# One quarter of every tile keeps its ninth product in PSUM, TensorE adds two planes to it and ScalarE takes it out; the hand-set course gets new places

## The reference, cut to what matters

```python
x = x + _L0_conv_ref(_gn(x), ...)      # x is 32 x 64 x 56 x 56, float32
x = x + _L1_conv_ref(_gn(x), W, b)

def _L0_conv_ref(x, dw_weight, ...):    # residual = x
    h = sign(x);  h = depthwise 3x3 conv with sign(dw_weight)
    h = sign(bn1(prelu1(h)));  h = 1x1 conv with sign(pw_weight)
    return bn2(prelu2(h)) + residual

def _L1_conv_ref(x, W, b):              # "involution", K = 3
    filters = einsum('bchw,oc->bohw', x, W) + b      # nine filters per channel and pixel
    patches = the nine 3x3 shifts of x
    return sum(patches * filters over the nine)
```

## Time and profile before

| what | number |
|---|---|
| median of three runs | 725.28 us (723.54 to 725.59) |
| the profiled execution, its time | 727.71 us |
| its span, first to last instruction | 725.8 us |
| DVE busy | 659.6 us, 91% |
| POOL busy | 636.0 us, 88% |
| PE busy | 608.0 us, 84% |
| ACT busy | 499.9 us, 69% |
| mean granted TensorE clock | 0.98 of full speed |

### The profile page before, as it was taken

How to read it: one execution, slowest core, us unless ns; L and a number is a source line. 1 busy time by engine, 2 the same in 40 slices (tenths; PEclk the granted TensorE clock), 3 DMA queues, 4 the chain that set the end, 5 groups by cost and what they waited for, 6 DMA issues and landing times.

```text
span 725.8 us, 18653 instructions
## 1 busy us (share of the span) xinstructions
PE 608.0 (84%) x8001; PEld 258.9 (36%) x8001; DVE 659.6 (91%) x984; ACT 499.9 (69%) x627; POOL 636.0 (88%) x330
## 2 busy tenths in 40 slices
PE   2649789889898988898898988888888889898777
PEld 1324333333334333343433333343333334342313
DVE  4939889999999999999999999999989999999986
ACT  6957896868778596868769696867849686735100
POOL 2003589999999999999999999999989999999997
PEclk9969999999999999999999999999999999999999
DMA  5246596998999899898989899898979987898974
GB/s 204 82 136 109 100 269 150 190 244 186 253 196 252 187 217 234 166 259 186 267 181 248 191 205 230 186 256 189 257 162 207 226 186 166 185 202 172 205 157 136
DMA packets 34279, 142.10 MB, mean 196 GB/s; under 512 B 3348, under 2 KB 11540, under 8 KB 32276
## 3 DMA queue, kind: packets, MB, share of 16 engines
q0 software_dynamic: 17232, 75.87, 58.7%
q1 hardware_dynamic: 16940, 65.03, 25.2%
q10 hardware_dynamic: 24, 0.00, 0.0%
HBM read 26.03 MB, written 25.69 MB: 71 GB/s over the span
## 4 chain that ended last, share of the span: by engine, by line
POOL 71%; issue 9%; DVE 9%; ACT 5%; PE 4%; DMA 1%; SPq 0%; POOLq 0%; DVEq 0%; ACTq 0%
POOL prod L402 29%; POOL ob L426 13%; POOL prod L415 11%; POOL prod L384 7%; POOL prod L408 7%; DVE prod L939 5%; POOL st L371 2%; PE tap_ps L498 2%; ACT unused L601 2%; PE tap_ps L520 1%; POOL st L369 1%; DVE xb L913 1%; DMA xb<-in_x_dram 1%; ACT ab L601 1%; ACT signs L601 1%
## 5 line engine op out<-in xcount | busy, mean ns | idle before, releaser
L498 PE MATMUL tap_ps<-q,w_t 64*64 64x392 f32 x2304 | 468.4, 504 | 57.7 <-DVE prod L939 31.4
L939 DVE SCALAR_TENSOR_TENSOR prod<-tap_ps,bias,q 128x784 f32<-128x784 f32 x493 | 486.0, 1025 | 32.7 <-PE tap_ps L498 21.3
L498 PE MATMUL tap_ps<-mirror,w_t 64*64 64x392 f32 x2304 | 462.9, 504 | 0.0
L498 PEld LDWEIGHTS tap_ps<-q,w_t 64*64 64x64 f32 x2304 | 154.9, 133 | 259.8 <-DVE prod L939 185.7
L402 POOL TENSOR_TENSOR prod<-prod 128x2352 f32<-128x2352 f32 x45 | 233.6, 5192 | 0.0
L601 ACT ACTIVATE ab<-tap_ps,col 128x784 bf16<-128x784 f32 x128 | 120.8, 995 | 57.0 <-PE tap_ps L541 56.3
L541 PE MATMUL tap_ps<-signs,dw_diag 64*64 64x392 bf16 x2304 | 135.2, 338 | 16.9 <-DVE prod L939 12.5
L498 PEld LDWEIGHTS tap_ps<-mirror,w_t 64*64 64x64 f32 x2304 | 139.3, 133 | 0.4 <-issue 0.4
L426 POOL TENSOR_TENSOR ob<-prod 128x784 f32<-128x784 f32 x63 | 133.0, 2111 | 4.3
L541 PEld LDWEIGHTS tap_ps<-signs,dw_diag 64*64 64x64 bf16 x2304 | 71.4, 109 | 106.6 <-issue 56.1
L384 POOL DMA_DIRECT2D prod<-prod x63 | 78.1, 1240 | 33.1 <-DVE prod L939 29.8
(11 more groups left out here) (115 smaller groups left out, 333.4 us busy)
## 6 DMA issues: line engine op xcount, KB each, us to landing
prod<-prod POOLq DMA_DIRECT2D x63, 1176.0 KB, 10.3
out_dram<-ob SPq DMA_DIRECT2D x31, 784.0 KB, 5.9
xb<-in_x_dram SPq DMA_DIRECT2D x15, 1568.0 KB, 12.4
mirror<-q SPq DMA_DIRECT2D x64, 203.0 KB, 4.5
xb<-in_x_dram SPq DMA_DIRECT2D x2, 784.0 KB, 5.8
out_dram<-ob SPq DMA_DIRECT2D x2, 392.0 KB, 2.3
prod<-in_L_conv_W_dram SPq DMA_DIRECT2D x1, 288.0 KB
prod<-in_L_conv_pw_weight_dram SPq DMA_DIRECT2D x1, 32.0 KB
```

The lines of the kernel that those rows point to most:

```text
L498: mm = pe.matmul(rows3(tap_ps[to, slot, side, 0:CH]), w_t[own, k, :], moving, start=True, stop=True)
L939: v.scalar_tensor_tensor(place.rearrange("p j (a b) -> p j a b", b=WD), psum.rearrange("p j (a b) -> p j a b", b=WD), s_(t, B4) if k == 4 ...
```

## The change

No function changes; constants do. Quarters 0, 1 and 2 are now on POOL, and quarter 3 takes the `in_banks` way (SUMMED). In tile 15 quarters 0 and 1 are in banks (SUMMED_LAST), and 2 and 3 stay kept. `in_banks` means: DVE writes the ninth product back into its slot, PE adds plane 7 at 11 units and plane 6 at 12 units after the quarter's start (`add_in_banks`: matmuls with the identity, two halves a plane, waiting for the quarter's ninth product), ACT takes the slot out with the mean added into plane 6 at 12 units (`take_from_banks`), and POOL does L408 and L426, but no L393. DVE does no `pair`. The slot is held until ACT has taken it. The four jobs, the statistics and the q passes get other places, `add_wide` and `add35` come one unit earlier (now ahead of the `fold` of two quarters on), `final` two units later (still behind it).

```diff
-POOLED = 1, 2, 3
-SUMMED = ()
-SUMMED_LAST = ()
+POOLED = 0, 1, 2
+SUMMED = 3,
+SUMMED_LAST = 0, 1
 BANK_DELAY = 11
-TAKE_DELAY = 13
+TAKE_DELAY = 12
-MEAN_DELAY = 12
-WIDE_ADD_DELAY = 21
-LATE_ADD_DELAY = 22
+MEAN_DELAY = 13
+WIDE_ADD_DELAY = 20
+LATE_ADD_DELAY = 21
-OUT_DELAY = 23
+OUT_DELAY = 25
 COURSE = {
- 'sum0': -74,
+ 'sum0': -73,
- 'sign0': -69,
- 'square0': -66,
- 'var0': -63,
- 'rstd0': -65,
+ 'sign0': -71,
+ 'square0': -67,
+ 'var0': -64,
+ 'rstd0': -66,
- 'inv_z': -56,
+ 'inv_z': -55,
- 'job0': -56,
+ 'job0': -50,
  'job1': -45,
- 'job2': -33,
- 'job3': -26,
- 'sum1': -16,
- 'mean1': -15,
+ 'job2': -30,
+ 'job3': -25,
+ 'sum1': -15,
+ 'mean1': -17,
- 'var1': -11,
- 'rstd1': -8,
+ 'var1': -12,
+ 'rstd1': -12,
  'q0': -11,
- 'q1': -3,
+ 'q1': -8,
 }
...
```

More of the change, by code:

```diff
@@ L1024 @@
      'square0': -67,
-     'var0': -66,
+     'var0': -67,
      'rstd0': -66,
@@ L1028 @@
      'inv_z': -60,
-     'ratio': -60,
+     'ratio': -58,
      'job0': -65,
@@ L1035 @@
      'mean1': -48,
-     'square1': -47,
+     'square1': -45,
      'var1': -45,
@@ L1048 @@
      'scales0': -78,
-     'inv_z': -36,
-     'ratio': -35,
-     'job0': -37,
-     'job1': -29,
+     'inv_z': -37,
+     'ratio': -33,
+     'job0': -39,
+     'job1': -32,
      'job2': -24,
@@ L1061 @@
      'q1': -7,
-     'inverse': -5},
- 2: {'sum0': -62,
+     'inverse': -2},
+ 2: {'sum0': -60,
      'mean0': -59,
@@ L1066 @@
      'square0': -53,
-     'var0': -49,
-     'rstd0': -51,
+     'var0': -48,
+     'rstd0': -48,
      'scales0': -46,
      'inv_z': -46,
-     'ratio': -44,
-     'job0': -42,
-     'job1': -37,
-     'job2': -32,
-     'job3': -27},
+     'ratio': -45,
+     'job0': -41,
+     'job1': -38,
+     'job2': -31,
+     'job3': -25},
 }
@@ L1082 @@
  'signs_rest': -43,
- 'square_0': -57,
+ 'square_0': -58,
  'square_1': -53,
```

## The result

The changed kernel takes 729.66 us (729.39 to 730.23), the kernel before, beside it on the same chip, 725.39. The ratio is 1.0062, 95% interval 1.0044 to 1.0081: slower by 4 us, where 709.5 was forecast. The span of the profiled execution is 727.5 us against 725.8.

A forecast was written before the change was run, and what follows sets the result against it. POOL was taken to bound, DVE 1.6 us behind. DVE's 38.7 + 1.1 + 0.3 + 0.5, less 0.2, gave 40.4 a tile against 41.3; with the ends, 18.3 us off 727.71, taken as 709.5, range 697 to 722.

The forecast's parts named there:

- POOL 37.7 to 39.5, DVE 38.7: Work per middle tile in us: POOL down from 41.35 by losing L393, DVE from 39.68 by losing a 0.95 pair.
- The adds, 1.1 and 0.3: PE's plane adds: DVE waits 1.1 us a tile at tap 40, then 0.3 more around the job at 42.
- Job 0's Relu, 0.5 (0 to 1): PE waits for job 0's Relu, queued in ACT between square and q halves; 0.5 us a tile reaches DVE.
- The 0.70 of the square goes: DVE's 0.70 us wait a tile, its shuffle waiting for ACT's square, should vanish with the moved places.
- That margin turns positive.: At a tile's start PE's 0.44 us wait for q's mirror ends, since its DMAs are issued some 2 us earlier.
- The step to tile 14, 0.3 saved: The step before the last tile, which has no statistics of a next tile, gains 0.3 us.
- The mirror ahead of tile 15, 0.9 saved: The 1.17 us wait for the mirror ahead of the last tile is mostly gone, saving 0.9.
- Tile 15, 2.0 saved: Last tile: two pairs (1.9 us) and POOL's 2.27 wait go, two banked quarters cost 1.1 each; 2.0 saved.
- The slow tile, 2.65: The one middle tile that lost 2.65 us, after a 2.49 us mirror wait and low clock, counted as saved.
- Rival 1: The adds hide: DVE waits 0.6 us a tile, not 1.7; 39.3 a tile, about 697 us; chance 0.20.
- Rival 2: PE's adds and Relu waits all reach DVE: 41.3 a tile, only the end gains; 723 us; chance 0.18.
- Rival 3: PE's wait at adds or mirror grows to 2.49 us every tile and the clock falls: 742 us; chance 0.06.

The follow-up runs named there:

- e14: Changed kernel with quarter 2's fold made small, copying one plane instead of three (two products left out): 715.57 us, ratio 0.9857.
- e3: Changed kernel without PE's matmuls that add plane 7 in banked quarters (one product left out of their sums): 714.91 us, ratio 0.9860.
- e2: Changed kernel with its new places, but quarter 3 and all of tile 15 kept, nothing in banks: 724.75 us, ratio 0.9988.
- e15: Changed kernel with POOL's root (L369, L371) moved ahead of quarter 2's fold in tiles 2 to 15: 758.08 us, ratio 1.0434.
- e17: Changed kernel with POOL's root ahead of quarter 2's fold, DVE's square shuffle one unit earlier, tile 15 all kept: 750.27 us, ratio 1.0342.
- e19: Changed kernel with quarter 2's fold in tiles 1 to 14 held until ACT has written the next q's first half: 742.07 us, ratio 1.0244.
- e7: Changed kernel with the first half of q put behind job 0's Relu in ACT's queue, from tile 2 on: 739.89 us, ratio 1.0182.

## Why the prediction was wrong, step by step

By the marks, 20 us lie between the forecast and the run: 12.8 in twelve tiles, 2.0 in the step to tile 14, 5.1 in the rest. Two steps failed in the middle. The wait at job 0's Relu was mis-sized (0.5 for 1.06, and nothing fell together; 8.2 us), and the mirror was taken to land earlier because it was issued earlier (4.6 us). The second failed again at the end, beside a banked quarter that the sum had left out.

- **"So now: POOL bounds, DVE is 1.6 us behind it, PE has some 5 us to spare."** Right for POOL, and incomplete. The DMA share of 0.93 stood in the earlier trace rows and no term of the sum was made of it. When a sixth of the folds' bytes was taken away, 0.65 us a tile and 4.6 at the end came out.
- **POOL 37.7 to 39.5, DVE 38.7.** Right: 38.5 and 38.8. POOL's waits moved to before the folds, where they were to be (10.8 us), and more of them to before L369 (17.5), which the prediction didn't name.
- **The adds, 1.1 and 0.3.** Measured 1.30 at product 40 in each tile, and 1.11 where the mirror is early (e14). That the wait is PE's lead running out is shown by e3 and by the runs in which a late mirror eats the lead. A good estimate.
- **Job 0's Relu, 0.5 (0 to 1).** Measured 1.06, just outside its bounds: the term was mis-sized, since I counted ACT's own work and not what ACT waits for. POOL issues the fold (1.21 us) ahead of the root, so ACT stood 1.03 us idle. Nor did the 0.2 "that falls together" fall together: the two waits are in series, 13 us apart. This is the larger miss of the middle: 40.37 became 41.05, 8.2 us in twelve tiles.
- **The 0.70 of the square goes.** Right, no such wait is left.
- **"That margin turns positive."** This is the step whose mechanism failed. I had the mirror issued about 2 us earlier and took its landing to move with it. It was issued 2.0 us earlier against the fold (4.8 us behind it, 6.8 before), and still lands 11.5 to 12.7 us behind the fold where PE waits for it. In early tiles that is just in time; later it costs PE 0.35 to 0.66 us (five times between 400 and 620) and a tile of 41.7 to 41.95 instead of 41.05, 4.6 us in all.
- **The step to tile 14, 0.3 saved.** It had no working. It took 41.69 and not 39.7: the waits of 1.03 and 1.30 are there as in every tile, and DVE's other wait for PE is 0.60.
- **The mirror ahead of tile 15, 0.9 saved.** It cost instead: PE waited 3.79 us there and DVE 2.10. The fold ahead of it was issued at 663.86 and PE's tap started at 675.36, 11.5 later.
- **Tile 15, 2.0 saved.** POOL's 2.27 went, and its two banked quarters cost 1.10 each, as counted. But the sum left out tile 14's banked quarter, whose adds also fall into tile 15. They came right behind the wait for the mirror and cost 1.63 and 1.30 (rows below). In e2, without banks but with the same mirror wait (2.13), the end is 4.3 us shorter.
- **The slow tile, 2.65.** No tile of the middle is slow after. This was right, but no step of the prediction says why. The wait of the earlier trace rows is not at the start of a tile but at its tap 18, the first that needs the second half of the mirror. Those two DMAs were issued at 512.38 and 513.82, behind the next tile's load of 1568 KB (509.24) on SP's queue, and the later one landed at 532.42. With `q1` five units earlier they go out ahead of the load (337.82 and 339.44, the load 340.16).
- **The rivals.** Rival 1's 697 is 699 by its own terms. Rival 2 (723, "PE takes what DVE and POOL give back") described the middle, though the cause is not PE's work alone: e14 has the same adds and a tile of 40.78. Rival 3 put its price on waits of 2.5 us a tile at the mirror. The changed kernel meets it once, in tile 15, and e15 waits 1.6 to 2.6 us in every tile and its clock falls to 0.50 in seven of twelve (758 us): the mechanism was real, its condition was not met. That it "decides from a wait near 2.5 us" was wrong: in e17 a wait of 1.29 us was followed by the low clock. What I lacked was a rival that ends at 730, with the mirror bound by the fold.

The rows of tile 15 in the kernel after (DVE, then PE), and windows over it:

```profile
676.50 1.03 DVE L939 SCALAR_TENSOR_TENSOR prod<-tap_ps,bias,q 128x784 f32<-128x784 f32 x1 [2.10 <-PE tap_ps L498]
...
681.68 1.03 DVE L939 SCALAR_TENSOR_TENSOR prod<-tap_ps,bias,q 128x784 f32<-128x784 f32 x1 [1.63 <-PE tap_ps L498]
684.01 1.03 DVE L939 SCALAR_TENSOR_TENSOR prod<-tap_ps,st,q 128x784 f32<-128x784 f32 x1 [1.30 <-PE tap_ps L498]
```
```profile
675.36 0.51 PE L498 MATMUL tap_ps<-q,w_t 64*64 64x392 f32 x1 [3.79 <-DMA mirror<-q]
```
```profile
670.00:671.00 1.00, 0.95 (x12) 0.21 (x8) 1.00 (x2) 1.00 (x3) 1.00 (x1) 1.00 1.22 212
675.40:677.40 2.00, 2.00 (x17) 1.02 (x21) 0.90 (x1) 0.00 (x0) 2.00 (x2) 0.65 0.54 96
677.40:680.40 3.00, 3.00 (x16) 1.17 (x8) 2.21 (x3) 0.00 (x0) 3.00 (x2) 0.66 1.07 191
```

The granted clock is 0.65 of full speed in the 5 us behind the long wait, 1.00 before it, so part of those microseconds ran at 1.2 and not at 2.4 GHz. That is the earlier trace rows again, and in part why these adds are dearer than the others. The other part is that PE had no lead behind its wait. The kernel before had a low clock at the same place (from 676.4 us), so the low clock there is not new.

What stays open: the kernel before was not run with the small fold, so how much of e14's 14 us is the fold's grip on this change, and how much any version would gain from it, isn't known. Nor do I know why the distance from fold to mirror grows over the tiles, 12.25 us at 260 us and 12.74 at 593. No version that leaves nothing out beat the kernel before beyond its uncertainty; the nearest is e2, 724.75 us, the new places without the banks.

## What to carry to other kernels

Add up the transfers of a round like the work of an engine. Take the share that their packets took, not the times to landing, which hold the waits behind one another. Over the whole kernel after it was:

```profile
q0 software_dynamic: 17232, 75.87, 56.5%
q1 hardware_dynamic: 16940, 65.03, 27.3%
```

In a tile of the middle it is 0.93, and that was the sign that a DMA on a critical edge may have to stand behind a big one. Cost an edge that ends in a DMA from the transfer in flight before it, not from its own issue. And ask of an engine with 5 us to spare whether it has them at the place of the new work; right behind a wait it has none.

## What was unexpected of the hardware

- A DMA of 203 KB issued by SP beside a fold of 1176 KB issued by POOL lands 11.4 to 12.7 us after the fold's issue, whether itself issued 2.6 or 4.8 us behind it; beside one of 392 KB its median is 3.1 us instead of 5.3. Nearly all of the difference lies ahead of its first packet (3.1 to 5.0 us behind the issue beside the large one, 1.25 beside the small). The Trainium skill ("DMA: Bandwidth & Descriptors", section on queues, rings and completion order) says that each DMA engine goes round its queues packet by packet, a packet being some 9 to 17 descriptors. The trace lists 256 pieces of 4704 bytes for a large fold, 16 for each of the 16 engines if they are dealt out evenly; if such a piece is a descriptor (neither is shown here), a whole fold would be about one turn, and the small transfer would have to wait for it as it does. The same section says that a completion increment lands only after every earlier write of that engine, across its queues; no run here shows how much of the landing that makes.
- A fold issued 3.8 us behind a load of 1568 KB, with another fold still under way (e19), took 16.6 us to be usable, against a median of 10.6. In the kernel after, the one issued 1.5 us behind that load (341.69) took 15.3.
- PE idle for 3.79 us left the clock at 0.65 for some 5 us; waits of 0.2 to 0.7 us left it at 1.00. In e15 a wait of 2.51 us (352.59) was followed by 1.00 too, and one of 2.28 (481.21) by 0.50, the windows here; in e17 one of 1.29 us was followed by 0.51 and one of 1.31 by 1.00. So the length of one wait alone doesn't decide. A tile that holds such a stretch takes 1.6 us more in e7 (43.3 against 41.65) and in e17 (43.5 against 41.85).

```profile
481.30:483.30 2.00, 2.00 (x16) 0.87 (x20) 0.35 (x1) 0.00 (x0) 2.00 (x2) 0.50 1.00 369
...
353.00:354.00 1.00, 1.00 (x20) 0.56 (x16) 0.36 (x1) 0.00 (x0) 1.00 (x2) 1.00 0.91 318
```

- POOL's issue of a DMA costs it time by size: 1.21 us for the large fold, 0.90 for the small. Where a short instruction stands behind it, that is on the path.
